# Cross attention of a two-layer decoder: the value products in two blocks a row, with eight exponential tiles, another order of the small products between the score rounds, and a last row on two score banks

## Chip, cores and metric

One core of one Trainium2 chip runs the whole program. The metric is device time in microseconds (us) of one execution. The kernel before took 1463.95 us (median of 3 runs, 1462.85 to 1476.16).

## What is computed

Two decoder layers over 16 batch rows of 112 tokens with 256 features. Each layer has a self attention (a different kind in each), a cross attention to a context of 375 x 128 a batch row, and a mixture of 8 experts. The change touches the cross attention alone, which runs once in each layer. Cut to what matters:

```python
qh = (layernorm(x) @ Wq + bq).reshape(B, 112, 16, 16)     # 16 heads of 16
kh = (ctx @ Wk + bk).reshape(B, 375, 16, 16)
vh = (ctx @ Wv + bv).reshape(B, 375, 16, 16)
attn = softmax(einsum('bqhd,bkhd->bhqk', qh, kh) / sqrt(16), axis=-1)
x = x + einsum('bhqk,bkhd->bqhd', attn, vh).reshape(B, 112, 256) @ Wo + bo
logits = layernorm(x) @ Wr + br                            # for the experts that follow
```

All of it is in float32.

## The kernel before

`cross_attention` (line 577) handles one batch row after another, t = 0 to 15, as a hand-written pipeline. Every engine has its own loop over t from -3 to 17 or so, and semaphores tie them together; what an engine does in a row stands in a fixed order, so an instruction that waits holds back all that is behind it on that engine.

The 16 heads of a row are taken in 8 slots of 2 heads. In each slot TensorE (PE) runs one *round* (`round_of`, L713): the two score products of a row ahead (`score`, L704, 112 x 375 into the bank pair `bsc`), from which VectorE (DVE) takes the maximum (`maximum`, L975); and the six products of the present row that compute the scores again, transposed and already shifted by that maximum (`shifted_score`, L710, into the bank pair `bp`), from which ScalarE (ACT) takes the exponential (`exps`, L892) into a tile `p`. Scores run 3 slots beyond a row ahead (`ahead`): slot 5 of row t has the first scores of row t + 2. There is one `bsc` and one `bp`, so a round waits until the maximum and the exponential of the round before have read them:

```python
reused(pe, exped, PAIRS * t + slot)      # L718
...
reused(pe, maxed, r - 1 if r < FILL else r)   # L725
```

Between two rounds stands a *gap* of other PE work, gap 0 behind round 0 and so on (L841 to L885). The value products of a row (`values`, L753: 12 small products for 4 heads, into `bo`) come in four blocks of one quad each; in gaps 2, 4 and 6 of their row and in gap 0 of the next, because there are only four `p` tiles. The other gap work is: the key projections `keys` (L785, two a row, bank `bk`), `queries` (L792, bank `bx`), the three `context_values` (L804), transposes of the normed row (`x_turn`, L761), of the negated maxima (`shift_turn`, L810), of the value sums (`u_turn`, L816), of the divided output (`out_turn`, L822) and of the new row (`row_turn`, L769), the output projection (`out_product`, L828) and the router's `logits` (L775). In gap 0 `keys` waits for `lg_set` (L781), which DVE raises in `row_logits` (L1038) when it has read the logits out of `bk`; in DVE's order that comes behind the first maximum of the row.

Three DMA transfers from SyncE (SP) join the engines: the keys of two rows ahead (`spread_k`, L653), the queries of two rows ahead (`spread_q`, L662 and L664, behind `q_copy`, L989, on DVE), whose end the round of slot 5 waits for (L721), and the negated maxima of the next row (`spread_nm`, L671), whose end round 0 of the next row waits for (L717).

In row 15 no scores are left, so a round has the six shifted products alone. Behind it, in t = 16 and 17, follow the last value block, the division, the output projection, the new row and its logits, and then the next phase.

Of the kernel before, what the change touches and what calls it, by code (L numbers as in the profile page):

```python
# [84 lines left out]
def reused(eng, sem, n):  # L85

    if not isinstance(n, int) or n > 0:
        eng.wait_ge(sem, n)
# [488 lines left out]
def cross_attention(nc, g, layer, xn_dram):  # L577
# [10 lines left out]
    qT = ph.sb("qT", [P, RB, QUADS, S])  # L588
    zeros = ph.sb("zeros", [4, QUADS, S])
    vb = ph.sb("v", [CT, VB, NC3, H, HD + 1])  # L590
    p = [ph.sb(f"p{u}", [CT, 2, NC3 * S]) for u in range(4)]
    mx = ph.sb("mx", [S, 2, 4, QUADS])
    nm = ph.sb("nm", [S, H])
    nmT = ph.sb("nmT", [H, 2, S])
# [33 lines left out]
    def on(b):  # L628
        return 0 <= b < NB
# [4 lines left out]
    def score_banks(b, pair):  # L634

        r = PAIRS * b + pair
        return bp if r < FILL and r % 2 else bsc

    def ahead(t, slot):
        return (t + 1, slot + 3) if slot < 5 else (t + 2, slot - 5)  # L640

    with nc.Block() as block:
# [53 lines left out]
        def _(pe):  # L696
# [10 lines left out]
            def shifted_score(b, pair, i, c):  # L707
                j, n = head(pair, i)
                r = 32 * j
                return pe.matmul(bp[0:CT, i, c * S:(c + 1) * S], kT[r:r + 32, b % RB, n, c * CT:(c + 1) * CT],  # L710
                                 qT[r:r + 32, b % RB, n, :], start=True, stop=True)

            def round_of(t, slot):  # L713
                sb, sp = ahead(t, slot)
                if on(t):
                    if slot == 0:
                        pe.wait_ge(nm_spread[t % RB], 16 * NM_DMAS * (t // RB + 1))  # L717
                    reused(pe, exped, PAIRS * t + slot)  # L718
                if on(sb):
                    if sp == 0:  # L720
                        pe.wait_ge(q_spread[sb % RB], 16 * Q_DMAS * (sb // RB + 1))  # L721
                    if sp % 4 == 0:
                        pe.wait_ge(k_spread[RB * (sp // 4) + sb % RB], 16 * K_DMAS * (sb // RB + 1))
                    r = PAIRS * sb + sp
                    reused(pe, maxed, r - 1 if r < FILL else r)  # L725
                if on(t):
                    for i in range(2):
                        shifted_score(t, slot, i, 0)
                if on(sb):
                    score(sb, sp, 0)  # L730
                    score(sb, sp, 1).then_inc(scored, 1)
                if on(t):
                    for c in range(1, NC3):
                        for i in range(2):
                            last = shifted_score(t, slot, i, c)
                    last.then_inc(shifted, 1)
                elif on(sb):
                    if sb == 0 and sp == 0:
                        pe.wait_ge(br_set, 1)
                    idle_products(bm[:, 0:P], 1)  # L740

            def values(b, n):
                pe.wait_ge(exped, PAIRS * b + 2 * n + 2)
                if n == 0:
                    reused(pe, u_copied, b)
                    pe.wait_ge(v_copied, NC3 * (b + 1))
                    if b == 0:
                        pe.wait_ge(set_v, 2 - layer)
                        pe.wait_ge(v_set, 1)
                for c in range(NC3):  # L750
                    for j in range(4):
                        slot = 2 * n + j // 2
                        last = pe.matmul(bo[32 * j:32 * j + HD + 1, n * S:(n + 1) * S], vb[:, b % VB, c, 4 * n + j, :],  # L753
                                         p[slot % 4][:, j % 2, c * S:(c + 1) * S], start=(c == 0), stop=(c == NC3 - 1))
                last.then_inc(valued, 1)

            def x_turn(b):
# [54 lines left out]
            def u_turn(b):  # L812
                pe.wait_ge(u_copied, b + 1)
                reused(pe, x_summed, b)
                for n in range(QUADS):
                    last = pe.transpose(bm[0:S, n * P:(n + 1) * P], uT[:, n * S:(n + 1) * S], g.ident[:, :])  # L816
                last.then_inc(u_turned, 1)
# [19 lines left out]

            if layer == 0:
                pe.wait_ge(g.cross_in, 16 * CROSS_DMAS)
            keys(0, 0)  # L840
            for t in range(-3, NB + 2):  # L841
                round_of(t, 0)
                if on(t - 1):
                    values(t - 1, 3)
                if on(t + 2) and t > -2:
                    keys(t + 2, 0)
                round_of(t, 1)
                if on(t + 2):
                    queries(t + 2)
                    if t == -2:  # L850
                        bias_rows()
                        idle_products(bp[:, 0, 0:P], 5 + 4 * layer)
                round_of(t, 2)
                if on(t):
                    values(t, 0)
                if on(t - 1):
                    u_turn(t - 1)
                round_of(t, 3)
                if on(t + 1):
                    context_values(t + 1, 0)  # L860
                    context_values(t + 1, 1)
                round_of(t, 4)
                if on(t):
                    values(t, 1)
                if on(t + 1):
                    context_values(t + 1, 2)
                round_of(t, 5)
                if on(t + 2):
                    keys(t + 2, 1)
                if on(t + 1):  # L870
                    shift_turn(t + 1)
                round_of(t, 6)
                if on(t):
                    values(t, 2)
                if on(t - 1):
                    out_turn(t - 1)
                if on(t - 2):
                    row_turn(t - 2)
                round_of(t, 7)
                if on(t + 3):  # L880
                    x_turn(t + 3)
                if on(t - 1):
                    out_product(t - 1)
                if on(t - 2):
                    logits(t - 2)  # L885

        @block.scalar
        def _(act):
            def exps(t, slot):
                act.wait_ge(shifted, PAIRS * t + slot + 1)  # L890
                reused(act, valued, 4 * t + slot // 2 - 1)
                act.activation(p[slot % 4][:, :, :], bp[0:CT, :, 0:NC3 * S], ACT.Exp).then_inc(exped, 1)  # L892

            def x_copy(b):
                act.wait_ge(x_turned, b + 1)
# [40 lines left out]
            for t in range(-3, NB + 2):  # L936
                if on(t):
                    exps(t, 0)
                if on(t - 1):
                    u_copy(t - 1)  # L940
                if on(t + 2):
                    k_copy(t + 2, 0)
                for slot in (1, 2, 3):
                    if on(t):
                        exps(t, slot)
                if on(t + 1):
                    v_copy(t + 1, 0)
                    v_copy(t + 1, 1)
                if on(t):
                    exps(t, 4)  # L950
                if on(t + 1):
                    v_copy(t + 1, 2)
                if on(t):
                    exps(t, 5)
                if on(t + 2):
                    k_copy(t + 2, 1)
                if on(t + 1):
                    shift_copy(t + 1)
                if on(t):
                    exps(t, 6)  # L960
                if on(t - 1):
                    out_copy(t - 1)
                if on(t - 2):
                    row_copy(t - 2)
                if on(t):
                    exps(t, 7)
                if on(t + 3):
                    x_copy(t + 3)

        @block.vector  # L970
        def _(dve):
# [73 lines left out]
            for t in range(-3, NB + 3):  # L1045
                for slot in range(8):
                    sb, sp = ahead(t, slot)
                    if on(sb):
                        maximum(sb, sp)
                    if slot == 0 and on(t - 3):  # L1050
                        row_logits(t - 3)
                    if slot == 0 and on(t - 2):
                        finish(t - 2)
                    if slot == 1 and on(t + 2):
                        q_copy(t + 2)
                        if t == -2:
                            bias_copies()
                    if slot == 2 and on(t - 1):
                        normalise(t - 1)
                    if slot == 3 and on(t - 2):  # L1060
                        second_norm(t - 2)
                    if slot == 4 and on(t + 1):
                        shift_rows(t + 1)
                    if slot == 6 and on(t + 3):
                        normed_row(t + 3)
                        if t == -3:
                            first_tiles()
# [900 lines left out]
```

## Time and profile before

| what | value |
|---|---|
| median of 3 runs | 1463.95 us (1462.85, 1463.95, 1476.16) |
| span of the profiled execution | 1473.2 us, TensorE clock 0.911 in the mean |
| its own time | 1476.16 us, the only one of the three above its span |
| cross attention of layer 0 | first round of row 0 at 197.2 us, last logits read at 491.9 us |
| cross attention of layer 1 | first round of row 0 at 972.1 us, last logits read at 1277.2 us |
| busy over the whole span | PE 89%, DVE 48%, ACT 38%, POOL 30% |

The span is the time from the first to the last instruction. A timeline row gives start, duration, engine, line, operation, tiles and count; what stands in brackets is how long the engine had stood idle and what ended that. One float32 product is two MATMUL records. PE records overlap, so a group's own duration says less than the distance from its start to the start of what follows.

### The profile page before, as it was taken

The page shows a single profiled execution, that of the slowest core. Times are in us where ns is not written, and L with a number is a line of the kernel's source. Part 1 is how long each engine was busy: PE and PEld are TensorE (multiplying, and loading weights), DVE is VectorE, ACT ScalarE, POOL GpSimd, SP SyncE. Part 2 cuts the span into 40 slices and gives each one's busy share as a digit, 9 for nine tenths or more (in the row PEclk, how much of TensorE's full clock was granted, in tenths as well). Part 3 has the DMA queues.
Part 4 walks back from the last instruction along what each step waited for, and adds up shares of the span by engine and source line. Part 5 has one row for each costly group of instructions (what it writes and reads, how often), then busy time and mean ns, then how long its engine had stood idle before and what let it go on. Part 6 is the DMA issues. An engine that isn't in the chain of part 4 may idle for free. (4 is left out here: it accounts for less than half of the span.)

```text
span 1473.2 us, 34595 instructions
## 1 busy us (share of the span) xinstructions
PE 1305.0 (89%) x13568; PEld 1036.2 (70%) x13568; DVE 701.9 (48%) x1744; ACT 558.2 (38%) x1246; POOL 444.8 (30%) x654
## 2 busy tenths in 40 slices
PE   5998899999998389999994999799999998559996
PEld 2665457777776279999993777557777776459996
DVE  4885345555552612222222999545565552323322
ACT  2776035555554012222221555135555553112221
POOL 5994300000000155556552221200000000135662
PEclk8999579999998589999997999799999997569999
DMA  7000111111110369999984000011111110279994
GB/s 241 2 2 2 23 26 36 36 36 37 36 36 17 128 225 340 346 347 337 329 320 107 1 1 1 15 29 42 44 44 43 42 43 25 80 192 347 356 368 147
DMA packets 61355, 177.89 MB, mean 121 GB/s; under 512 B 20608, under 2 KB 41953, under 8 KB 46756
## 3 DMA queue, kind: packets, MB, share of 16 engines
q0 software_dynamic: 22176, 141.55, 27.0%
q1 hardware_dynamic: 39044, 34.46, 9.2%
q8 instruction: 95, 1.56, 0.4%
q14 instruction: 40, 0.33, 0.1%
HBM read 147.62 MB, written 12.85 MB: 109 GB/s over the span
## 5 line engine op out<-in xcount | busy, mean ns | idle before, releaser
L975 DVE TENSOR_REDUCE xa_mx<-xa_ps_s 112x2 f32<-112x750 f32 x246 | 231.5, 941 | 219.4 <-PE xa_ps_s L704 215.9
L892 ACT ACTIVATE xa_p<-xa_ps_p 125x672 f32<-125x672 f32 x256 | 187.2, 731 | 236.2 <-PE xa_ps_p L710 236.2
L710 PEld LDWEIGHTS xa_ps_p<-xa_qT,xa_kT 32*125 32x125 f32 x3072 | 199.4, 191 | 95.3 <-ACT xa_p L892 66.8
L710 PE MATMUL xa_ps_p<-xa_qT,xa_kT 32*125 32x112 f32 x3072 | 243.4, 291 | 24.4 <-DVE xa_mx L975 10.4
L704 PE MATMUL xa_ps_s<-xa_kT,xa_qT 32*112 32x375 f32 x984 | 224.8, 534 | 1.0 <-DMA xa_qT<-xa_qU 1.0
L1803 PEld LDWEIGHTS ex_ps_h<-ex_xT,ew_w 128*128 128x128 f32 x1792 | 213.7, 196 | 4.8 <-issue 2.0
L1803 PE MATMUL ex_ps_h<-ex_xT,ew_w 128*128 128x128 f32 x1792 | 214.3, 279 | 1.3 <-ACT ex_xT L1833 1.3
L1814 PE MATMUL ex_ps_y<-ew_w,ex_hT 128*128 128x256 f32 x896 | 202.7, 379 | 0.0
L1814 PEld LDWEIGHTS ex_ps_y<-ew_w,ex_hT 128*128 128x128 f32 x896 | 165.9, 190 | 20.2
L1837 ACT ACTIVATE ex_hT<-ex_ps_h,ew_w 128x128 f32<-128x128 f32 x224 | 70.1, 364 | 282.5 <-PE ex_ps_h L1803 282.5
L1849 DVE TENSOR_SCALAR ex_hT<-ex_ps_h,ew_w 128x128 f32<-128x128 f32 x224 | 68.2, 346 | 163.7 <-PE ex_ps_h L1803 163.7
L1090 POOL TENSOR_SCALAR rstd<-mv 112x1 f32<-112x1 f32 x32 | 7.1, 221 | 418.5 <-DVE mv L1015 418.5
L753 PE MATMUL xa_ps_o<-xa_p,xa_v 125*17 125x112 f32 x3072 | 103.5, 270 | 0.0
L571 POOL TENSOR_TENSOR line_inv<-line_ss,nhalf 112x32 f32<-112x32 f32 x16 | 87.7, 5478 | 9.5 <-DVE line_ss L476 9.3
L753 PEld LDWEIGHTS xa_ps_o<-xa_p,xa_v 125*17 125x17 f32 x3072 | 68.9, 100 | 14.7 <-issue 1.2
L785 PE MATMUL xa_ps_k<-cT,wk_x 128*128 128x375 f32 x128 | 60.7, 558 | 15.3 <-DVE lg L1038 11.0
L704 PEld LDWEIGHTS xa_ps_s<-xa_kT,xa_qT 32*112 32x112 f32 x984 | 68.7, 174 | 5.0 <-issue 3.5
L1095 POOL TENSOR_TENSOR x<-x,crow 112x256 f32<-112x256 f32 x16 | 11.6, 726 | 191.2 <-DVE xa_xn L178 191.2
L1868 DVE TENSOR_TENSOR ex_y<-ex_ps_y,ew_w 128x256 f32<-128x256 f32 x35 | 14.8, 424 | 109.0 <-PE ex_ps_y L1814 89.5
L1740 POOL DMA_INDIRECT ex_xg<-xn,ex_now x56 | 55.7, 994 | 23.1 <-issue 21.4
L903 ACT ACTIVATE xa_kU<-xa_ps_k,bk_x 128x375 f32<-128x375 f32 x64 | 36.7, 574 | 48.4 <-PE xa_ps_k L785 48.3
L1833 ACT ACTIVATE ex_xT<-ex_ps_t 128x256 f32<-128x256 f32 x56 | 21.5, 384 | 79.9 <-PE ex_ps_t L1791 79.9
(304 smaller groups left out, 2000.0 us busy)
## 6 DMA issues: line engine op xcount, KB each, us to landing
xa_kT<-xa_kU SPq DMA_DIRECT2D x128, 93.8 KB, 2.2
xa_qT<-xa_qU SPq DMA_DIRECT2D x64, 56.0 KB
xn<-xa_x SPq DMA_DIRECT2D x32, 112.0 KB, 2.2
lin_yg<-ys SPq DMA_DIRECT2D x16, 224.0 KB, 5.2
cT<-in_ctxT SPq DMA_DIRECT2D x4, 750.0 KB, 8.3
xa_qT<-xa_nmT SPq DMA_DIRECT2D x128, 1.8 KB
x<-in_x SPq DMA_DIRECT2D x4, 448.0 KB, 6.2
xn<-x SPq DMA_DIRECT2D x16, 112.0 KB, 2.1
```

Source lines behind the costliest of these rows:

```text
L571: pool.tensor_tensor(inv[:, b % 2], ss[:, b % 2], g.nhalf[:, :], ALU.pow).then_inc(inv_done, 1)
L704: return pe.matmul(score_banks(b, pair)[0:S, i, 0:CL], qT[r:r + 32, b % RB, n, :], kT[r:r + 32, b % RB, n, :], start=True, stop=True)
L710: return pe.matmul(bp[0:CT, i, c * S:(c + 1) * S], kT[r:r + 32, b % RB, n, c * CT:(c + 1) * CT], qT[r:r + 32, b % RB, n, :], start=True, s ...
L753: last = pe.matmul(bo[32 * j:32 * j + HD + 1, n * S:(n + 1) * S], vb[:, b % VB, c, 4 * n + j, :], p[slot % 4][:, j % 2, c * S:(c + 1) * S] ...
L785: pe.matmul(bk[:, 0:CL], g.wk_x[:, layer, m * P:(m + 1) * P], g.cT[:, b, :], start=True, stop=True).then_inc(k_made, 1)
L892: act.activation(p[slot % 4][:, :, :], bp[0:CT, :, 0:NC3 * S], ACT.Exp).then_inc(exped, 1)
L975: dve.tensor_reduce(mx[:, b % 2, j:j + 2, n], score_banks(b, pair)[0:S, :, 0:CL], AX, ALU.max).then_inc(maxed, 1)
L1740: pool.indirect_dma_start(xg[:, slot, :], None, xn_dram, bass.IndirectOffsetOnAxis(ap=now[:, slot, 0:1], axis=0)) \
L1803: last = pe.matmul(bh[k][:, (j % 2) * SLOTS:(j % 2 + 1) * SLOTS], w[:, u, (1 - c) * FF + j * P:(1 - c) * FF + (j + 1) * P], xT[:, 1 - c, : ...
L1814: last = pe.matmul(by[u % 2][:, 0:D], hT[:, u % 2, j, :], w[:, u, 2 * FF + FJ + j * D:2 * FF + FJ + (j + 1) * D], start=(j == 0), stop=(j ...
L1837: last = act.activation(hT[:, u % 2, 2 * k + i, :], bh[k][:, i * SLOTS:(i + 1) * SLOTS], ACT.Relu, bias=bias(u, 2 * k + i))
L1849: last = dve.tensor_scalar(hT[:, u % 2, 2 * k + i, :], bh[k][:, i * SLOTS:(i + 1) * SLOTS], bias(u, 2 * k + i), 0.0, ALU.add, ALU.max)
```

## The change

- There are eight `p` tiles, one for each slot, so `values` and `exps` use `p[slot]`, and an exponential waits for the value products of the row before in its slot.
- The four value blocks of a row come in two pairs: quads 0 and 1 in gap 6 of the row, quads 2 and 3 in gap 1 of the next.
- The rest is spread over the other six gaps: `keys(t+2, 0)` and `x_turn(t+2)` in gap 0 (the transpose was in gap 7 for row t + 3), `queries` in gap 2 (was 1), `u_turn` in gap 4 (was 2), `shift_turn`, `keys(t+2, 1)` and `out_turn` in gap 5 (`out_turn` was in 6), `row_turn` in gap 6, `out_product` and `logits` in gap 7. ACT's copies follow in that order.
- DVE does `row_logits` ahead of the first maximum of a row, `q_copy` in slot 2 (was 1), `normalise` in slot 4 (was 2).
- Row 15 has an order of its own (`last_row`): its rounds use `bp` and `bsc` in turn, and come in pairs.

```diff
-    p = [ph.sb(f"p{u}", [CT, 2, NC3 * S]) for u in range(4)]
+    p = [ph.sb(f"p{u}", [CT, 2, NC3 * S]) for u in range(PAIRS)]
...
+    def shift_banks(b, pair):
+
+        return bsc if b == NB - 1 and pair % 2 else bp
...
-                    reused(pe, exped, PAIRS * t + slot)
+                    if t < NB - 1 or slot == 0:
+                        reused(pe, exped, PAIRS * t + slot)
+                    elif slot == 1:
+                        pe.wait_ge(maxed, PAIRS * NB)
+                    else:
+                        pe.wait_ge(exped, PAIRS * t + slot - 1)
...
+            def last_row(t):
+                round_of(t, 0)
+                round_of(t, 1)
+                values(t - 1, 2)
+                values(t - 1, 3)
+                round_of(t, 2)
+                round_of(t, 3)
+                values(t, 0)
+                u_turn(t - 1)
...
                 round_of(t, 0)
-                if on(t - 1):
-                    values(t - 1, 3)
                 if on(t + 2) and t > -2:
                     keys(t + 2, 0)
+                if on(t + 2):
+                    x_turn(t + 2)
                 round_of(t, 1)
+                if on(t - 1):
+                    values(t - 1, 2)
+                    values(t - 1, 3)
+                round_of(t, 2)
                 if on(t + 2):
                     queries(t + 2)
...
                 round_of(t, 6)
                 if on(t):
-                    values(t, 2)
-                if on(t - 1):
-                    out_turn(t - 1)
+                    values(t, 0)
+                    values(t, 1)
...
-                reused(act, valued, 4 * t + slot // 2 - 1)
-                act.activation(p[slot % 4][:, :, :], bp[0:CT, :, 0:NC3 * S], ACT.Exp).then_inc(exped, 1)
+                reused(act, valued, 4 * (t - 1) + slot // 2 + 1)
+                act.activation(p[slot][:, :, :], shift_banks(t, slot)[0:CT, :, 0:NC3 * S], ACT.Exp).then_inc(exped, 1)
...
+                    if slot == 0 and on(t - 3):
+                        row_logits(t - 3)
                     if on(sb):
                         maximum(sb, sp)
-                    if slot == 0 and on(t - 3):
-                        row_logits(t - 3)
```

On PE, from gap 7 of a row in the middle of layer 0 to gap 1 of the next, before (the three rows `xa_ps_p`, `xa_ps_s`, `xa_ps_p` are a round; a group's name says what it writes and from what):

```order
L761 MATMUL xa_ps_x<-ident,xa_xn 128x112 x2
L828 MATMUL xa_ps_m<-wo_x,xa_aoT 112x256 x2
L775 MATMUL xa_ps_k<-wr,xa_x2T 112x8 x2
L710 MATMUL xa_ps_p<-xa_qT,xa_kT 125x112 x2
L704 MATMUL xa_ps_s<-xa_kT,xa_qT 112x375 x2
L710 MATMUL xa_ps_p<-xa_qT,xa_kT 125x112 x4
L753 MATMUL xa_ps_o<-xa_p,xa_v 17x112 x12
L785 MATMUL xa_ps_k<-cT,wk_x 128x375
L710 MATMUL xa_ps_p<-xa_qT,xa_kT 125x112 x2
L704 MATMUL xa_ps_s<-xa_kT,xa_qT 112x375 x2
L710 MATMUL xa_ps_p<-xa_qT,xa_kT 125x112 x4
L792 MATMUL xa_ps_x<-xa_xT,wq_x 128x112 x4
```

and the same stretch of the changed kernel:

```order
L837 MATMUL xa_ps_m<-wo_x,xa_aoT 112x256 x2
L784 MATMUL xa_ps_k<-wr,xa_x2T 112x8 x2
L714 MATMUL xa_ps_p<-xa_qT,xa_kT 125x112 x2
L708 MATMUL xa_ps_s<-xa_kT,xa_qT 112x375 x2
L714 MATMUL xa_ps_p<-xa_qT,xa_kT 125x112 x4
L794 MATMUL xa_ps_k<-cT,wk_x 128x375
L770 MATMUL xa_ps_x<-ident,xa_xn 128x112 x2
L714 MATMUL xa_ps_p<-xa_qT,xa_kT 125x112 x2
L708 MATMUL xa_ps_s<-xa_kT,xa_qT 112x375 x2
L714 MATMUL xa_ps_p<-xa_qT,xa_kT 125x112 x4
L762 MATMUL xa_ps_o<-xa_p,xa_v 17x112 x24
```

The transpose into `xa_ps_x` moved from gap 7 into gap 0, the value block left gap 0, a double one stands in gap 1, and the queries left gap 1.

On DVE, from the last slot of such a row to slot 3 of the next, before (`xa_mx` is the maximum, `lg` the logits, `xa_qU` the queries, `xa_rs` and `xa_ao` the division):

```order
L975 TENSOR_REDUCE xa_mx<-xa_ps_s 112x2 x2
L1038 TENSOR_TENSOR lg<-xa_ps_k,xa_brb 112x8
L1011 TENSOR_TENSOR x<-x,xa_ps_m 112x256
L1013 BN_STATS xa_stats<-x 112x6
L1015 BN_AGGR mv<-xa_stats 112x2
L975 TENSOR_REDUCE xa_mx<-xa_ps_s 112x2
L989 SCALAR_TENSOR_TENSOR xa_qU<-xa_ps_x,xa_bqs 128x224
L975 TENSOR_REDUCE xa_mx<-xa_ps_s 112x2
L1002 RECIPROCAL xa_rs<-xa_ps_m 112x16
L1004 TENSOR_TENSOR xa_ao<-xa_ps_m,xa_rs 112x256
```

and now:

```order
L1005 TENSOR_REDUCE xa_mx<-xa_ps_s 112x2
L1068 TENSOR_TENSOR lg<-xa_ps_k,xa_brb 112x8
L1005 TENSOR_REDUCE xa_mx<-xa_ps_s 112x2
L1041 TENSOR_TENSOR x<-x,xa_ps_m 112x256
L1043 BN_STATS xa_stats<-x 112x6
L1045 BN_AGGR mv<-xa_stats 112x2
L1005 TENSOR_REDUCE xa_mx<-xa_ps_s 112x2 x2
L1019 SCALAR_TENSOR_TENSOR xa_qU<-xa_ps_x,xa_bqs 128x224
```

The logits are read one maximum earlier, and the queries are copied one maximum later.

On PE, row 15 of layer 0, from its first round on, before (x6 is a round without scores):

```order
L710 MATMUL xa_ps_p<-xa_qT,xa_kT 125x112 x6
L753 MATMUL xa_ps_o<-xa_p,xa_v 17x112 x12
L710 MATMUL xa_ps_p<-xa_qT,xa_kT 125x112 x12
L753 MATMUL xa_ps_o<-xa_p,xa_v 17x112 x12
L816 MATMUL xa_ps_m<-ident,xa_uT 112x128 x4
```

and now:

```order
L714 MATMUL xa_ps_p<-xa_qT,xa_kT 125x112 x6
L714 MATMUL xa_ps_s<-xa_qT,xa_kT 125x112 x6
L762 MATMUL xa_ps_o<-xa_p,xa_v 17x112 x24
L714 MATMUL xa_ps_p<-xa_qT,xa_kT 125x112 x6
L714 MATMUL xa_ps_s<-xa_qT,xa_kT 125x112 x6
L762 MATMUL xa_ps_o<-xa_p,xa_v 17x112 x12
L825 MATMUL xa_ps_m<-ident,xa_uT 112x128 x4
```

Two rounds go to two banks back to back, where each waited for the exponential of the one before.

## Rows read from the trace of the kernel before

**Rows 1.** The page: busy time of each engine, and the group of the value products.

```profile
PE 1305.0 (89%) x13568; PEld 1036.2 (70%) x13568; DVE 701.9 (48%) x1744; ACT 558.2 (38%) x1246; POOL 444.8 (30%) x654
...
L753 PE MATMUL xa_ps_o<-xa_p,xa_v 125*17 125x112 f32 x3072 | 103.5, 270 | 0.0
```

**Rows 2.** Timeline of row 7 of layer 0: PE and DVE.

```profile
319.99 0.36 PE L710 MATMUL xa_ps_p<-xa_qT,xa_kT 32*125 32x112 f32 x2
...
322.09 0.87 PE L785 MATMUL xa_ps_k<-cT,wk_x 128*128 128x375 f32 x2 [0.50 <-DVE lg L1038]
...
322.89 0.36 PE L710 MATMUL xa_ps_p<-xa_qT,xa_kT 32*125 32x112 f32 x2
...
323.73 1.15 PE L792 MATMUL xa_ps_x<-xa_xT,wq_x 128*128 128x112 f32 x8
323.84 0.94 DVE L975 TENSOR_REDUCE xa_mx<-xa_ps_s 112x2 f32<-112x750 f32 x1 [0.89 <-PE xa_ps_s L704]
...
324.91 0.39 DVE L989 SCALAR_TENSOR_TENSOR xa_qU<-xa_ps_x,xa_bqs 128x224 f32<-128x224 f32 x1
324.93 0.36 PE L710 MATMUL xa_ps_p<-xa_qT,xa_kT 32*125 32x112 f32 x2
...
325.76 0.77 PE L753 MATMUL xa_ps_o<-xa_p,xa_v 125*17 125x112 f32 x24
...
326.46 0.65 PE L816 MATMUL xa_ps_m<-ident,xa_uT 128*112 128x128 f32 x4
327.04 0.36 PE L710 MATMUL xa_ps_p<-xa_qT,xa_kT 32*125 32x112 f32 x2
...
330.62 0.70 PE L804 MATMUL xa_ps_x<-wv_x,cT 128*125 128x256 f32 x2
...
331.24 0.36 PE L710 MATMUL xa_ps_p<-xa_qT,xa_kT 32*125 32x112 f32 x2
...
332.08 0.90 PE L785 MATMUL xa_ps_k<-cT,wk_x 128*128 128x375 f32 x2
...
332.82 0.26 PE L810 MATMUL xa_ps_x<-ident,xa_nm 112*16 112x112 f32 x1
...
333.28 0.36 PE L710 MATMUL xa_ps_p<-xa_qT,xa_kT 32*125 32x112 f32 x2 [0.20 <-DVE xa_mx L975]
...
334.82 0.41 PE L822 MATMUL xa_ps_m<-ident,xa_ao 112*128 112x112 f32 x2
...
335.35 0.36 PE L710 MATMUL xa_ps_p<-xa_qT,xa_kT 32*125 32x112 f32 x2
...
336.44 1.03 PE L828 MATMUL xa_ps_m<-wo_x,xa_aoT 128*112 128x256 f32 x4
...
337.70 0.36 PE L710 MATMUL xa_ps_p<-xa_qT,xa_kT 32*125 32x112 f32 x2
```

**Rows 3.** Timeline of SP: issues of the query transfers in rows 6 and 7.

```profile
308.23 2.01 SPq L664 DMA_DIRECT2D xa_qT<-xa_qU  x2
...
325.94 1.29 SPq L664 DMA_DIRECT2D xa_qT<-xa_qU  x2
```

**Rows 4.** The tile of the keys: its transfers, from issue to landing.

```profile
DMA to landing us min/median/max: 2.0/2.2/3.3
```

**Rows 5.** Timeline of row 15 in both layers: first round, last value block.

```profile
460.19 0.91 PE L710 MATMUL xa_ps_p<-xa_qT,xa_kT 32*125 32x112 f32 x12
...
479.43 1.32 PE L753 MATMUL xa_ps_o<-xa_p,xa_v 125*17 125x112 f32 x24
...
1240.24 1.60 PE L710 MATMUL xa_ps_p<-xa_qT,xa_kT 32*125 32x112 f32 x12
...
1264.73 1.32 PE L753 MATMUL xa_ps_o<-xa_p,xa_v 125*17 125x112 f32 x24
```

**Rows 6.** Stretches: busy time of PE, PEld, DVE, ACT, POOL; granted clock; DMA.

```profile
462.00:485.00 23.00, 18.84 (x206) 14.43 (x207) 3.12 (x10) 7.50 (x13) 1.23 (x3) 0.66 0.04 11
...
1245.00:1275.00 30.00, 23.68 (x201) 18.17 (x201) 4.62 (x15) 6.76 (x12) 1.56 (x4) 0.50 0.06 16
```

More of the change, by code:

```diff
@@ L709, in shifted_score @@
                 r = 32 * j
-                return pe.matmul(bp[0:CT, i, c * S:(c + 1) * S], kT[r:r + 32, b % RB, n, c * CT:(c + 1) * CT],
+                return pe.matmul(shift_banks(b, pair)[0:CT, i, c * S:(c + 1) * S], kT[r:r + 32, b % RB, n, c * CT:(c + 1) * CT],
                                  qT[r:r + 32, b % RB, n, :], start=True, stop=True)
@@ L753, in values @@
                         last = pe.matmul(bo[32 * j:32 * j + HD + 1, n * S:(n + 1) * S], vb[:, b % VB, c, 4 * n + j, :],
-                                         p[slot % 4][:, j % 2, c * S:(c + 1) * S], start=(c == 0), stop=(c == NC3 - 1))
+                                         p[slot][:, j % 2, c * S:(c + 1) * S], start=(c == 0), stop=(c == NC3 - 1))
                 last.then_inc(valued, 1)
@@ L839, in _ @@
                 pe.wait_ge(g.cross_in, 16 * CROSS_DMAS)
+            def last_row(t):
[7 more added lines that the diff above has]
+                u_turn(t - 1)
+                round_of(t, 4)
+                round_of(t, 5)
+                values(t, 1)
+                out_turn(t - 1)
+                row_turn(t - 2)
+                round_of(t, 6)
+                round_of(t, 7)
+                out_product(t - 1)
+                logits(t - 2)
             keys(0, 0)
             for t in range(-3, NB + 2):
+                if t == NB - 1:
+                    last_row(t)
+                    continue
                 round_of(t, 0)
-                if on(t - 1):
-                    values(t - 1, 3)
                 if on(t + 2) and t > -2:
                     keys(t + 2, 0)
+                if on(t + 2):
+                    x_turn(t + 2)
                 round_of(t, 1)
+                if on(t - 1):
+                    values(t - 1, 2)
+                    values(t - 1, 3)
+                round_of(t, 2)
                 if on(t + 2):
@@ L852, in _ @@
                         idle_products(bp[:, 0, 0:P], 5 + 4 * layer)
-                round_of(t, 2)
-                if on(t):
-                    values(t, 0)
-                if on(t - 1):
-                    u_turn(t - 1)
                 round_of(t, 3)
@@ L862, in _ @@
                 round_of(t, 4)
-                if on(t):
-                    values(t, 1)
+                if on(t - 1):
+                    u_turn(t - 1)
                 if on(t + 1):
@@ L867, in _ @@
                 round_of(t, 5)
+                if on(t + 1):
+                    shift_turn(t + 1)
                 if on(t + 2):
                     keys(t + 2, 1)
-                if on(t + 1):
-                    shift_turn(t + 1)
+                if on(t - 1):
+                    out_turn(t - 1)
                 round_of(t, 6)
                 if on(t):
-                    values(t, 2)
-                if on(t - 1):
-                    out_turn(t - 1)
+                    values(t, 0)
+                    values(t, 1)
                 if on(t - 2):
@@ L879, in _ @@
                 round_of(t, 7)
-                if on(t + 3):
-                    x_turn(t + 3)
                 if on(t - 1):
@@ L938, in _ @@
                     exps(t, 0)
+                if on(t + 2):
+                    k_copy(t + 2, 0)
+                    x_copy(t + 2)
+                if on(t):
+                    exps(t, 1)
                 if on(t - 1):
                     u_copy(t - 1)
-                if on(t + 2):
-                    k_copy(t + 2, 0)
-                for slot in (1, 2, 3):
+                for slot in (2, 3):
                     if on(t):
@@ L954, in _ @@
                     exps(t, 5)
+                if on(t + 1):
+                    shift_copy(t + 1)
                 if on(t + 2):
                     k_copy(t + 2, 1)
-                if on(t + 1):
-                    shift_copy(t + 1)
                 if on(t):
@@ L966, in _ @@
                     exps(t, 7)
-                if on(t + 3):
-                    x_copy(t + 3)
         @block.vector
@@ L1047, in _ @@
                     sb, sp = ahead(t, slot)
+                    if slot == 0 and on(t - 3):
+                        row_logits(t - 3)
                     if on(sb):
                         maximum(sb, sp)
-                    if slot == 0 and on(t - 3):
-                        row_logits(t - 3)
                     if slot == 0 and on(t - 2):
                         finish(t - 2)
-                    if slot == 1 and on(t + 2):
+                    if slot == 2 and on(t + 2):
                         q_copy(t + 2)
@@ L1057, in _ @@
                             bias_copies()
-                    if slot == 2 and on(t - 1):
-                        normalise(t - 1)
                     if slot == 3 and on(t - 2):
@@ L1063, in _ @@
                         shift_rows(t + 1)
+                    if slot == 4 and on(t - 1):
+                        normalise(t - 1)
                     if slot == 6 and on(t + 3):
```

## Prediction

> **What bounds the kernel now.** I read the page first, then the stretches, then the timeline of one row, then the tails of the phase and the transfers. The page has PE busy in 89% of the span and the next engine, DVE, in 48% [rows 1]; PE records overlap, so that is no proof that PE sets the pace of the cross attention. The timeline of row 7 does that. The row lasts 337.70 - 319.99 = 17.71 us [rows 2]. In two slots the next round comes 2.04 us after the one before (322.89 to 324.93, 331.24 to 333.28), and the second of these says what PE waited for: the maximum on DVE, 0.20. The loop is: round start, 0.95 until the maximum starts (322.89 to 323.84), 0.94 of maximum, 0.15 until PE goes on. With one bank pair for scores no slot can be shorter, so the floor of a row is 8 x 2.04 = 16.32 us. The row is 17.71 - 16.32 = 1.39 above it. Where: a gap begins 0.84 after its round (322.89 to 323.73), so gap work up to 1.20 is free and what is over it is paid. Gap 0 pays 2.90 - 2.04 = 0.86 (a value block, then `keys`, which stood idle 0.50 for the logits to be read on DVE). Gap 2 pays 0.07 (324.93 to 327.04), gaps 3 and 4 together 0.12 (327.04 to 331.24), gap 6 0.03, gap 7 0.31 (335.35 to 337.70).
>
> **The row, gap by gap.** The pieces, start to start [rows 2]: a value block 0.70 (325.76 to 326.46), `u_turn` 0.58, the third context product 0.62, a key projection 0.74 (332.08 to 332.82), `shift_turn` 0.26 (0.46 to the round less 0.20 of waiting), `out_turn` and `row_turn` together 0.53 (334.82 to 335.35), `out_product` with `logits` 1.26 (336.44 to 337.70). A transpose pair, `x_turn` too, I put at half of 0.53, 0.27.
>
> A pair of value blocks is not in the trace. The block's group lasts 0.77 and one of its products 0.27 [rows 1, 2], so the last of 24 records starts 0.50 after the first, and the 0.20 from there to the next instruction is what a change of form costs. A second block of the same form could then start after 0.52, and the pair takes 0.52 + 0.70 = 1.22; I take 1.24. The other end is two full blocks, 1.40.
>
> - Gap 0: 0.74 + 0.27 = 1.01, free: 2.04. The wait for the logits goes, because DVE reads them ahead of the maximum of slot 0, some 0.9 earlier, while PE is in round 0. `keys` is late next, behind its own round.
> - Gap 1: 0.84 + 1.24 = 2.08. DVE's sums of slot 0 follow the maximum as before and now end close to the next maximum; I add 0.01 for them: 2.09.
> - Gap 2, `queries`: 2.04, as it had in gap 1. Gap 3 unchanged: 2.04. Gap 4: 0.84 + 0.58 + 0.62 = 2.04.
> - Gap 5: 0.84 + 0.26 + 0.74 + 0.27 = 2.11. Gap 6: 0.84 + 1.24 + 0.27 = 2.35. Gap 7: 0.84 + 1.26 = 2.10.
>
> Sum: 2.04 x 4 + 2.09 + 2.11 + 2.35 + 2.10 = 16.81, against 17.71: 0.90 a row. Rows 3 to 12 of both layers have this pattern, 20 x 0.90 = 18.0. Rows 0 to 2 and 13 lack parts of the work that is moved; for these 8 I take half, 3.6. Together 21.6 us. With pairs of 1.40 it would be 0.32 x 28 = 9.0 less.
>
> The ACT and DVE orders I cost at nothing. ACT is busy in 38% of the span [rows 1], its copies stand between two exponentials as before, at most two in a slot, and where a round waited in row 7 it was for DVE, not for ACT [rows 2]; without that cover a late exponential would hold the next round by what it is late. `normalise` on DVE, now behind the maximum of slot 4, has 2.04 - 0.94 = 1.10 until the next maximum, and if it needed more, it is the maximum of slot 5 that would start late. The eight `p` tiles add a wait on value products that ended a slot or more before. The transfer of the negated maxima is issued earlier in the row, as `shift_turn` stands first in gap 5 and the key copy behind it.
>
> **The edit that adds a risk.** The queries move one slot later, but the round of slot 5 waits for their transfer as before; behind that wait stand all of PE's rounds. `q_copy` starts 1.18 after the queries (323.73 to 324.91) [rows 2], now 0.84 + 1.18 = 2.02 after round 2. Round 5 comes 3 x 2.04 = 6.12 after round 2, so 4.10 is left from `q_copy` to the landing; before it was 331.24 - 324.91 = 6.33. The first of the two query transfers is issued 1.03 after `q_copy` (325.94), the second half of 1.29 later, at 1.68 [rows 3]. The trace gives no landing for them; the keys' transfers take 2.0 to 3.3, 2.2 in the middle [rows 4]. So the landing is at 3.7 to 5.0, most likely 3.9: 0.2 to spare, or at the worst 0.9 late in each of 28 rows, 25 us. I take the middle, since most transfers lie near it, with 2 us for the late ones (row 6 issued its pair in 2.01 instead of 1.29, 0.7 later).
>
> **Row 15.** From its first round to its last value block layer 0 took 479.43 - 460.19 = 19.24 and layer 1 1264.73 - 1240.24 = 24.49 [rows 5]. A round of six products took 0.91 at first in layer 0 and 1.60 in layer 1, a value block 1.32 at both ends against 0.77 in row 7: the granted clock is 0.66 in the first tail and 0.50 in the second [rows 6], that is 1.2 GHz in part of the one and in all of the other. Now: four pairs of rounds, each 0.64 + 0.84 = 1.48, 5.9; three value stretches, 1.24 + 0.70 + 0.70, and 0.52 to the last block, 3.2; `u_turn` 0.58, the transposes 0.53, projection and logits 1.26. That is 11.4 of PE work at 2.4 GHz, and I add 1.5 for waits on exponentials and copies: 12.9. At 1.2 GHz PE work grows by 1.60 / 0.91 = 1.76, to 20, and hides the waits. So layer 0 gains between 6.3 and -0.8 (I take 4) and layer 1 in this execution between 11.6 and 4.5 (I take 7).
>
> **Sum.** Profiled execution: 21.6 - 2 + 4 + 7 = 30.6, from 1476.2 to 1445.6. The median lies 12.2 below it, and 5.2 of that may be the slow tail of layer 1 (24.49 - 19.24); for the median I take 4 for that tail as well: 21.6 - 2 + 4 + 4 = 27.6, 1463.95 - 27.6 = 1436. That is what I predict; its own range is 1428 to 1446.
>
> **The rivals.**
> 1. *The pair of blocks saves no change of form* (1.40): 9 us less, 1445. For it: no such pair stands in the trace. Against: inside a block the records start about 0.02 apart.
> 2. *The queries land late.* For it: only 0.2 to spare. Against: the middle landing fits. With 0.5 in every row 14 us instead of 2 go, 1448.
> 3. *The clock falls earlier in the tail.* Row 14 has no keys and no queries left, so its gaps 0 and 2 are now empty, where before gap 0 still had a value block; layer 1's tail stood at 1.2 GHz [rows 6]. Then row 15 gains nothing over layer 0's 19.24 (-0.8 each instead of 4), and row 14 takes up to 5 longer in each layer (as layer 1's row 15 did): 19.6 - 11.6 = 8, 1456. The Trainium skill ("TensorE: Matmul & The Clock Gate", section "Why this matters for your kernels") says that idle gaps between bursts of products send the clock to half. By that rule this rival would be the likely one, with its 1456. Against it stands row 7, where a value block takes 0.77, the speed of 2.4 GHz, with waits of 0.2 to 0.5 around it: short waits alone do not do it.
> 4. *Slower.* If the query pair is issued as in row 6 (0.7 later) and lands as the slowest of the key transfers (3.3), round 5 waits 5.7 - 4.1 = 1.6 in 28 rows, 45 us: 1463.95 - 29.6 + 45 = 1479. It decides from a wait of about 1.05 in every row, where all other gains are eaten. Against it: the slow issue is one row of many.
>
> That the change does not do what it says can be left out: the order of PE shows it.
>
> **Chances.** Forecast 0.61, rival 1 0.10, rival 2 0.12, rival 3 0.13, rival 4 0.04. About 1% (14.6 us) is what a measurement here can tell from no change, so faster means under 1449. The forecast and rival 1 count as faster, and about two thirds of rival 2: 0.79. Rival 3 and the rest of 2 are within 1%: 0.17. Rival 4 is slower: 0.04. The range, 1420 to 1457, reaches from a median run with both tails at full clock and no late landing (29.6 - 8 + 12.6 = 34 gained) and some 10 more for what I left out, to rival 3.
>
> **What would show it.** Row 7 of layer 0 lasts 16.8; no PE wait on the reading of the logits; slot 5 without an idle time ended by the query transfer; a group of 48 value records followed after 1.24; gap 6 the longest, 2.35; row 15 in about 13 where the clock is full. A row near 17.3 with waits on the transfer in slot 5 would be rival 2; rows of 16.8 with a total near 1455 would be rival 3.

## The result, and the profile after

The changed kernel took 1410.53 us (median of 5 runs, 1405.75 to 1427.47), the kernel before 1465.19 (median of 5, 1462.85 to 1476.16). The ratio is 0.963, 95% interval 0.960 to 0.967, a gain of some 54 us. Ratios compare, here and below, those runs of each kernel that lie within 1.5% of its fastest. The forecast was 1436.0 with a range from 1420 to 1457: the direction was right, and the gain about twice the 28 forecast. The time lies below the range.

The profiled execution of the changed kernel took 1427.47 us, with a span of 1425.8. It is the longest of its five, as the profiled execution before (1476.16) is the longest of its own, and both have their filling ahead of row 0 of layer 0 at 1.2 GHz (the last part below), so the two profiles are like with like: 1473.2 - 1425.8 = 47.4 us of span. The page, busy time of each engine and the group of the value products, answers to [rows 1]:

```profile
PE 1264.5 (89%) x13568; PEld 1023.8 (72%) x13568; DVE 701.8 (49%) x1744; ACT 555.1 (39%) x1246; POOL 445.6 (31%) x654
...
L762 PE MATMUL xa_ps_o<-xa_p,xa_v 125*17 125x112 f32 x3072 | 86.4, 260 | 0.0
```

As many instructions are run (x13568, x1744, x1246), PE is busy 40 us less, and its share of the span is 89% in both. The page alone says nothing of where the time went. The timeline of PE, DVE and SP in row 7 of layer 0, beside [rows 2, 3], says it for a row:

```profile
318.34 0.36 PE L714 MATMUL xa_ps_p<-xa_qT,xa_kT 32*125 32x112 f32 x2
...
318.44 0.17 DVE L1068 TENSOR_TENSOR lg<-xa_ps_k,xa_brb 112x8 f32<-112x8 f32 x1 [0.41 <-PE xa_ps_k L784]
...
319.17 0.90 PE L794 MATMUL xa_ps_k<-cT,wk_x 128*128 128x375 f32 x2
...
320.37 0.36 PE L714 MATMUL xa_ps_p<-xa_qT,xa_kT 32*125 32x112 f32 x2
...
321.21 1.34 PE L762 MATMUL xa_ps_o<-xa_p,xa_v 125*17 125x112 f32 x48
...
322.48 0.36 PE L714 MATMUL xa_ps_p<-xa_qT,xa_kT 32*125 32x112 f32 x2
...
324.50 0.39 DVE L1019 SCALAR_TENSOR_TENSOR xa_qU<-xa_ps_x,xa_bqs 128x224 f32<-128x224 f32 x1
324.52 0.36 PE L714 MATMUL xa_ps_p<-xa_qT,xa_kT 32*125 32x112 f32 x2
...
325.53 1.28 SPq L668 DMA_DIRECT2D xa_qT<-xa_qU  x2
...
328.58 0.36 PE L714 MATMUL xa_ps_p<-xa_qT,xa_kT 32*125 32x112 f32 x2
...
330.62 0.36 PE L714 MATMUL xa_ps_p<-xa_qT,xa_kT 32*125 32x112 f32 x2
...
331.45 1.34 PE L762 MATMUL xa_ps_o<-xa_p,xa_v 125*17 125x112 f32 x48
...
333.07 0.36 PE L714 MATMUL xa_ps_p<-xa_qT,xa_kT 32*125 32x112 f32 x2
...
335.26 0.36 PE L714 MATMUL xa_ps_p<-xa_qT,xa_kT 32*125 32x112 f32 x2
```

The row lasts 335.26 - 318.34 = 16.92. The logits are read at 318.44, ahead of the maximum, and the keys at 319.17 start without an idle time. The pair of value blocks is followed by the next round 1.27 after its start. Round 5 at 328.58 stands without an idle time too, 4.08 after the copy of the queries: no wait on their transfer in this row. Over the rows of both layers PE does wait for it three times, 2.2 us in all and 1.4 at the longest; before, no round of a row did:

```profile
PE xa_ps_p L714 <- DMA xa_qT<-xa_qU: 2.2, 3, 1.4
```

Gap 6 (2.45) and gap 7 (2.19) are the two long ones.

The stretches of the two tails say where the larger part went. Columns: busy time of PE, PEld, DVE, ACT, POOL, granted clock (1.00 is 2.4 GHz, 0.50 is 1.2 GHz), DMA share, GB/s. Before, row 14 and row 15 of layer 0, then of layer 1 (row 15 here to the end of its last value block):

```profile
443.80:460.19 16.39, 14.14 (x236) 11.02 (x235) 6.89 (x13) 8.04 (x15) 0.79 (x2) 1.00 0.11 28
460.19:480.75 20.56, 17.82 (x233) 13.96 (x232) 3.22 (x11) 7.10 (x11) 0.79 (x2) 0.72 0.02 6
1219.44:1240.24 20.80, 18.55 (x237) 14.15 (x236) 6.89 (x13) 8.15 (x15) 0.78 (x2) 0.77 0.13 33
1240.24:1266.06 25.82, 23.32 (x233) 18.28 (x232) 3.20 (x11) 7.11 (x11) 0.77 (x2) 0.50 0.04 10
```

After, row 14 of layer 0, then row 15 and what follows it up to the last logits, layer 0 and layer 1:

```profile
436.82:453.27 16.45, 13.73 (x236) 11.13 (x236) 6.89 (x13) 8.14 (x15) 0.79 (x2) 1.00 0.07 18
453.27:465.21 11.94, 11.18 (x257) 9.39 (x256) 3.31 (x11) 6.45 (x11) 0.79 (x2) 1.00 0.05 12
465.21:474.28 9.07, 4.00 (x23) 2.99 (x22) 2.78 (x9) 1.51 (x4) 1.58 (x4) 0.91 0.09 25
...
1208.44:1220.38 11.94, 11.18 (x257) 9.38 (x256) 3.30 (x11) 6.45 (x11) 0.77 (x2) 1.00 0.09 24
1220.38:1230.70 10.32, 5.27 (x22) 3.80 (x22) 2.77 (x9) 1.51 (x4) 1.57 (x4) 0.65 0.15 44
```

Row 15 took 20.56 and 25.82 at a clock of 0.72 and 0.50, and takes 11.94 at 1.00 in both layers: it never leaves 2.4 GHz now. A pair of its rounds, from the first round to the value products behind the second, takes 454.43 - 453.27 = 1.16:

```profile
453.27 0.58 PE L714 MATMUL xa_ps_p<-xa_qT,xa_kT 32*125 32x112 f32 x6
...
454.43 1.34 PE L762 MATMUL xa_ps_o<-xa_p,xa_v 125*17 125x112 f32 x48
```

Summed over the two profiles, both layers:

| stretch | before | after | gain |
|---|---|---|---|
| rows 3 to 12 | 177.10, 177.10 | 169.35, 169.47 | 15.4 |
| rows 0 to 2 and 13 | 69.48, 70.28 | 68.94, 68.96 | 1.9 |
| row 14 | 16.39, 20.80 | 16.45, 16.44 | 4.3 |
| row 15 | 20.56, 25.82 | 11.94, 11.94 | 22.5 |
| from there to the last logits | 11.16, 11.14 | 9.06, 10.32 | 2.9 |
| filling ahead of row 0 | 44.15, 30.08 | 44.18, 28.82 | 1.2 |

That is 48 us, and outside the cross attention each stretch is within 1.3 us of before. Of it 17.3 come from the rows and 30 from the tail (rows 14, 15 and what follows).

### The profile page after: what moved, and what is told of

Its sections match the earlier page's. It is cut to its first block and busy times, and to the rows that moved or that the text cites. A ratio compares the mean times of both kernels' runs of the same rounds, so it can differ in the third digit from the quotient of the medians.

```text
span 1425.8 us, 34587 instructions
## 1 busy us (share of the span) xinstructions
PE 1264.5 (89%) x13568; PEld 1023.8 (72%) x13568; DVE 701.8 (49%) x1744; ACT 555.1 (39%) x1246; POOL 445.6 (31%) x654
## 5 line engine op out<-in xcount | busy, mean ns | idle before, releaser
L921 ACT ACTIVATE xa_p<-xa_ps_p 125x672 f32<-125x672 f32 x248 | 181.3, 731 | 212.2 <-PE xa_ps_p L714 212.2
L714 PE MATMUL xa_ps_p<-xa_qT,xa_kT 32*125 32x112 f32 x2976 | 227.1, 282 | 25.7 <-DVE xa_mx L1005 10.5
L714 PEld LDWEIGHTS xa_ps_p<-xa_qT,xa_kT 32*125 32x125 f32 x2976 | 187.4, 184 | 77.2 <-ACT xa_p L921 59.3
L762 PE MATMUL xa_ps_o<-xa_p,xa_v 125*17 125x112 f32 x3072 | 86.4, 260 | 0.0
L1125 POOL TENSOR_TENSOR x<-x,crow 112x256 f32<-112x256 f32 x16 | 11.6, 725 | 181.7 <-DVE xa_xn L178 181.7
```

The source lines that it names most:

```text
L714: return pe.matmul(shift_banks(b, pair)[0:CT, i, c * S:(c + 1) * S], kT[r:r + 32, b % RB, n, c * CT:(c + 1) * CT], qT[r:r + 32, b % RB, n, ...
L921: act.activation(p[slot][:, :, :], shift_banks(t, slot)[0:CT, :, 0:NC3 * S], ACT.Exp).then_inc(exped, 1)
```

## The experiments

**e1: the change without its last row.** Row 15 keeps the changed order of all other rows, on one bank.

```diff
-        return bsc if b == NB - 1 and pair % 2 else bp
+        return bp
...
-                if t == NB - 1:
-                    last_row(t)
-                    continue
```

> The changed kernel with row 15 in the general order and on one score bank, so the new order of rows 0 to 14 alone. Theory A (the tail gives the part that was not forecast, because row 15 on two banks is short and stays at 2.4 GHz): row 15 takes 16 to 20 instead of 11.9 from its first round to the end of its last value product, and the clock falls inside it or before; 1420 at the least, 1430 to 1436 if the clock falls as in the kernel before. Theory B (the extra gain lies in the rows or outside the cross attention): within 5 of the changed kernel's 1411.

Measured: 1446.08 (median of 4), ratio 0.983, 0.974 to 0.992. Rows 3 to 12 take 169.43 and 169.28, as in the changed kernel; row 15 takes 24.60 and 22.27:

```profile
437.21:461.81 24.60, 21.84 (x257) 17.29 (x256) 3.47 (x12) 7.00 (x11) 1.58 (x4) 0.62 0.02 6
1223.52:1245.79 22.27, 19.51 (x257) 15.59 (x256) 3.30 (x11) 7.00 (x11) 1.27 (x4) 0.69 0.05 13
```

The row gain stands by itself, and without the two banks row 15 falls to 1.2 GHz for part of its length; it first falls 2.4 us behind the first round in layer 0 and 8.0 us behind it in layer 1. So theory A holds, but both numbers were missed: row 15 is longer than the 16 to 20 expected, and the time is above 1430 to 1436. The timeline of its first rounds shows the wait that the two banks take away, an empty gap in which PE stands until the exponential has read the one bank:

```profile
437.21 0.91 PE L714 MATMUL xa_ps_p<-xa_qT,xa_kT 32*125 32x112 f32 x12
...
438.94 1.03 PE L714 MATMUL xa_ps_p<-xa_qT,xa_kT 32*125 32x112 f32 x12 [0.83 <-ACT xa_p L913]
```

PE stands idle for 24.60 - 21.84 = 2.76 there in all; in the changed kernel it is 11.94 - 11.18 = 0.76. Row 14 is the same in both, with an idle time of 16.45 - 13.73 = 2.72, and stays at 1.00 in both.

**e2: the last row alone.** The rows 0 to 14 in the order of before, with eight `p` tiles and row 15 on two banks in pairs (against the kernel before):

```diff
+            def last_row(t):
+                round_of(t, 0)
+                round_of(t, 1)
+                values(t - 1, 3)
+                round_of(t, 2)
+                round_of(t, 3)
+                values(t, 0)
+                u_turn(t - 1)
...
```

> The kernel before with eight exponential tiles and the new row 15 (two banks, rounds in pairs), its old order in rows 0 to 14. Theory A: rows 3 to 12 stay at 17.71, row 15 takes about 12 and the tail gains 18 to 26 of the 54 us: 1439 to 1447. Theory B: at most the 9 us that the two banks are worth at an equal clock: 1456 or more.

Measured: 1440.65 (median of 4), ratio 0.984, 0.974 to 0.993. Rows 3 to 12 take 177.12 and 177.11, as before. Row 15, in both layers:

```profile
445.75:458.16 12.41, 11.21 (x233) 9.23 (x232) 3.23 (x11) 6.46 (x11) 0.79 (x2) 1.00 0.04 11
1211.04:1223.44 12.40, 11.19 (x233) 9.22 (x232) 3.21 (x11) 6.45 (x11) 0.77 (x2) 1.00 0.10 30
```

So the two parts add up: by the ratios e1 gains 25 us and e2 24 on 1468.31, each give or take 13 or so, and the change 54. Within these intervals each part carries about half; the two profiles above give 17 us to the rows and 30 to the tail. The eight tiles cost nothing that shows in rows 3 to 12.

**e3: the logits behind the first maximum again**, all else as changed.

```diff
-                    if slot == 0 and on(t - 3):
-                        row_logits(t - 3)
                     if on(sb):
                         maximum(sb, sp)
+                    if slot == 0 and on(t - 3):
+                        row_logits(t - 3)
```

> The changed kernel with DVE reading the logits behind the first maximum of a row again, nothing else. If the wait on the logits in gap 0 was worth what the row's sum says, the keys start 0.5 to 1.3 later in gap 0 and rows 3 to 12 take 17.4 to 18.1 instead of 16.93: 15 to 30 us slower than the changed kernel. If the wait is hidden in the new order: 16.93 and no difference.

Measured: 1431.98 (one run). Rows 3 to 12 take 180.10 and 181.21, more than the 177.10 of before; row 15 stays at 11.94. The timeline of slot 0 of row 7, PE and DVE:

```profile
305.78 0.36 PE L714 MATMUL xa_ps_p<-xa_qT,xa_kT 32*125 32x112 f32 x2
...
306.73 0.94 DVE L1005 TENSOR_REDUCE xa_mx<-xa_ps_s 112x2 f32<-112x750 f32 x1 [1.25 <-PE xa_ps_s L708]
307.58 0.16 DVE L1068 TENSOR_TENSOR lg<-xa_ps_k,xa_brb 112x8 f32<-112x8 f32 x1
...
307.88 0.87 PE L794 MATMUL xa_ps_k<-cT,wk_x 128*128 128x375 f32 x2 [1.20 <-DVE lg L1068]
...
308.88 0.36 PE L714 MATMUL xa_ps_p<-xa_qT,xa_kT 32*125 32x112 f32 x2
```

Nothing stands ahead of the keys in gap 0 any more, so the whole wait shows: 1.20 idle, and the slot takes 3.10 instead of 2.03. In the new order one small instruction on DVE, moved past one maximum, is worth 18.07 - 16.94 = 1.1 us a row (the means over rows 3 to 12 of both layers), more than the whole row gain.

**e4: the kernel before, with the logits first.** The same two statements of before, exchanged.

```diff
-                    if on(sb):
-                        maximum(sb, sp)
                     if slot == 0 and on(t - 3):
                         row_logits(t - 3)
+                    if on(sb):
+                        maximum(sb, sp)
```

> The kernel before, with DVE reading the logits ahead of the first maximum of a row, nothing else. If that order is the main gain of a row: gap 0 falls from 2.90 to 2.3 to 2.4 and rows 3 to 12 take 17.1 to 17.2 instead of 17.71, 5 to 6 us a layer, 10 to 12 us in all (1452 to 1458 against 1465). If the placing of the value blocks is the gain of a row and the logits matter only in the new order: 17.5 to 17.7.

Measured: 1451.24 (median of 10, 1438.84 to 1473.50 and one of 2400.36 that nothing here explains), ratio 0.989, 0.984 to 0.994. Rows 3 to 12 take 172.55 and 172.90, 17.27 a row against 17.71, between the two expectations; slot 0 of row 7 is 2.37 instead of 2.90, and the keys follow the value block without an idle time:

```profile
304.71 0.36 PE L710 MATMUL xa_ps_p<-xa_qT,xa_kT 32*125 32x112 f32 x2
...
305.55 0.77 PE L753 MATMUL xa_ps_o<-xa_p,xa_v 125*17 125x112 f32 x24
...
306.25 0.90 PE L785 MATMUL xa_ps_k<-cT,wk_x 128*128 128x375 f32 x2
...
307.08 0.36 PE L710 MATMUL xa_ps_p<-xa_qT,xa_kT 32*125 32x112 f32 x2
```

So 4.4 of the 7.7 us that a layer's rows 3 to 12 gain come from these two lines in the old order already; the remaining 3.3, a third of a microsecond a row, are the pairs and the moved work. Row 15 (24.07 and 20.05, clock 0.56 and 0.74) gains nothing. The ratio stands for 9 to 23 us, and rows 3 to 12 of both layers make 8.8 of them.

**e5: one bank, with the empty gaps filled.** As e1, but in the empty gaps of rows 14 and 15 PE multiplies the identity into a bank that nobody reads at that point, so the result is untouched.

```diff
+            FILLS = {(NB - 2, 0): 4, (NB - 2, 2): 4, (NB - 1, 0): 3, (NB - 1, 2): 3, (NB - 1, 3): 3, (NB - 1, 4): 1, (NB - 1, 5): 2}
...
+                    idle_products(bsc[:, 0, 0:P], n)
...
```

> The row order of the changed kernel with the general order and one score bank in row 15 (as in the run of the general last row), and products of the identity whose results nobody reads in the empty gaps of rows 14 and 15; they leave the computation as it is. If PE's activity decides the clock there: 2.4 GHz until the end of row 15, which takes 16 to 17 instead of 22 to 25 with one bank, 12 to 16 us less than that run and still 8 to 10 more than the changed kernel. If the two banks themselves were the gain and the clock falls anyway: 22 to 25 and no gain.

Measured: 1419.41 (median of 4), ratio 0.972, 0.963 to 0.982. Row 15 in both layers:

```profile
434.76:451.55 16.79, 16.79 (x281) 14.10 (x280) 3.32 (x11) 6.99 (x11) 0.79 (x2) 1.00 0.04 10
1194.33:1211.12 16.79, 16.79 (x281) 14.11 (x280) 3.30 (x11) 6.99 (x11) 0.77 (x2) 1.00 0.06 17
```

PE has no idle time left and stays at 2.4 GHz, with the same bank, the same rounds and the same exponentials as e1. So PE's idle time is what let the clock fall. e5 fills gaps of row 14 too and does not part the two rows; but row 14 is unfilled in the changed kernel and in e1 alike, and only e1, with the waits of row 15 behind it, loses the clock. It also splits the gain of row 15: from e1's 24.60 and 22.27 to 16.79 is the clock, 7.8 and 5.5; from 16.79 to 11.94 is what the two banks and the pairs save at full clock, 4.85 (at most: the filling may overrun a gap; up to the fifth round it does not, as the rounds start 1.74, 3.85, 5.59 and 7.33 behind the first in e5 and in layer 1 of e1, which has 1.00 until then). Twice 4.85 is about the 9 us by which e5 is longer than the changed kernel. Against e1 it is 26.7 us shorter, more than the 12 to 16 expected: row 15 accounts for 13.3, the stretch behind it for 3.3, and the profiled execution of e1 has a long filling in layer 1 (last part), that of e5 has none.

**e6: two identity products in each filling round**, where the changed kernel has one, to hold the clock ahead of row 0.

```diff
-                    idle_products(bm[:, 0:P], 1)
+                    idle_products(bm[:, 0:P], 2)
```

> The changed kernel with two identity products instead of one behind each round of the fill ahead of row 0. If the spread of the runs is the clock in the two fills (28 to 30 us each at 2.4 GHz, 43 to 44 at 1.2): both fills at 28 to 31 in most runs, 1400 to 1408 and a smaller spread. If the clock there does not follow this work: the same spread and 1 to 4 us slower.

Measured: 1409.97 (median of 6, 1408.24 to 1416.02), ratio 0.965, 0.959 to 0.970; both fillings take 30 us (29.87 and 30.20). None of the six runs is near 1427, but four of the five runs of the changed kernel are as short, and the 1400 to 1408 expected were not reached. It is not shown to be faster than the changed kernel.

**e0 and e7: the two kernels once more.**

> The kernel before, once more with a profile. If its tail at 1.2 GHz is its rule and not a mishap of one execution, layer 1's row 15 again takes 24 to 26 from its first round to the end of its last value product, and layer 0's 19 to 26. If the first profile was an exception, 15 to 17 in both.

> The changed kernel once more with a profile. Row 15 at 11.9 in both layers and 2.4 GHz as before, rows 3 to 12 at 16.93; the fills at 28 to 44, apart from each other and from the first profile.

Measured: 1473.24 and 1412.78 (one run each). e0 has its long filling in layer 1 and not in layer 0:

```profile
155.18:185.99 30.81, 28.40 (x121) 16.06 (x121) 15.64 (x24) 4.73 (x12) 12.42 (x24) 0.81 0.12 28
933.79:977.35 43.56, 41.12 (x123) 21.77 (x124) 15.19 (x22) 4.38 (x11) 8.55 (x12) 0.54 0.10 22
```

Its row 15 takes 23.83 and 23.23, at a clock of 0.58 and 0.60: a little under the 24 to 26 expected of layer 1, and nowhere near 15 to 17, so the long tail is no exception. e7 has neither filling long (27.97 and 29.23), rows 3 to 12 at 169.39 and 169.44, and row 15 at 11.95 and 11.94. The tails of rows 14, 15 and what follows, both layers together, take 102.2 in e0 and 75.3 in e7: 27 us, where the two profiles gave 30.

## Why the prediction was right and wrong

- *The row.* Right in its working: 16.92 against 16.81 forecast, 0.77 gained a row against 0.90. The wait for the logits is gone, and e4 and e3 show that it was the largest single cause. The pair of value blocks takes 1.27 against 1.24, which refutes the first rival (1.40). The misses are gap 6, 2.45 against 2.35, gap 7, 2.19 against 2.10, and on the other side gap 5, 2.04 against 2.11. Rows 0 to 2 and 13 were taken at 3.6 and gave 1.9.
- *The queries.* The distance from the copy to round 5 was worked out as 4.10 and is 4.08, and in most rows nothing waits. A few transfers are late, as the prediction took it for 2 us: 2.2 us of waiting in the changed kernel, 0.4 to 2.3 in e1, e3, e5, e6 and e7. The longest waits, 1.4 in e3 and 1.65 in e6, are about the 1.6 of the fourth rival, but in one row of many and not in every one, so the second and the fourth rival do not happen.
- *The step that failed* is row 15: "layer 0 gains between 6.3 and -0.8 (I take 4) and layer 1 in this execution between 11.6 and 4.5 (I take 7)". The mechanism, pairs of rounds on two banks, was right. Wrong was the clock: I took a value between the two levels, as if the shorter row would run part of its length at 1.2 GHz as the longer one had. But the change takes away the idle time itself, 2.7 us of it down to 0.8, and e1 and e5 show that the clock hangs on it. All ten tails with the two-bank row (after, e2, e3, e6, e7) have row 15 at a clock of 1.00, in 11.94 to 12.41; all eight with one bank and empty gaps (before, e0, e1, e4) at 0.50 to 0.74, in 20 to 26. The end at 2.4 GHz was mis-sized as well: 12.9 to the start of the last value block, measured 11.2 (11.94 to the block's end). A pair of rounds was put at 1.48, with a 0.64 that no row shows, and takes 1.16; the waits, put at 1.5, are 0.76. In the two profiles the tail gave 30 us where 11 were taken: 7 more by the clock in row 15, 3.4 more by its work, and some 8 by what was put at nothing, row 14, the last value block and the stretch behind it. e0 and e7 give 27, where the forecast of the median took 8. With 27 in place of 8, and the rows at 17.3 for 19.6, the forecast would have been 1463.95 - 27.6 - 19 + 2.3 = 1420.
- *The third rival* had the same mechanism with the opposite sign. It feared the emptier gaps of row 14, and row 14 stays at 1.00 in both layers (16.45 and 16.44). The Trainium skill ("TensorE: Matmul & The Clock Gate", section "Why this matters for your kernels") warns of idle gaps between bursts of products, but of longer ones than the waits of these rows, 1.1 us at the most, so it did not make this rival the likely one. That several short waits can do it, other than I read from row 7, is what e1 and e5 show: 22.3 to 24.6 at 0.69 and 0.62 with the waits, 16.79 at 1.00 without. I looked for idle time only where the change adds it, and not where it takes it away.
- *The rest of the distance* is in the comparison of profile and median. I put part of the 12.2 us between them to the slow tail of layer 1, and took 3 less for the median's tail. The size was right, 105.9 for both tails in the first profile against 102.2 in e0, but it left the rest unexplained, and in e0 both layers have a long row 15 (23.83 and 23.23), so such a tail is nothing special to one execution. What differs more from one execution to the next, in both kernels, is the filling ahead of row 0 (last part). With a long one the profile of the changed kernel stands 16 us above the next longest of its runs.
- *The range* went down to "both tails at full clock", but priced that at 12.6 us, from layer 0's row 15 twice, and counted neither row 14 of layer 1 (4.4) nor the stretch behind row 15 (2.9).

What stays open: the last 9 us, from that 1420 to 1410.5 (the long filling may come more often before the change than after it; the profiles, with 2 long ones of 8 in the old order of the rows and 2 of 12 in the new, don't settle it); why row 14 falls to 0.77 in layer 1 of one execution of before and to 0.9 in both layers of e2 (18.08 and 17.94, with row 15 behind it at 1.00), and stays at 1.00 in e1, e7 and after; and which part of gaps 6 and 7 is the price of standing behind a pair.

## What to carry to other kernels

Where the granted clock falls in a stretch, ask first whether the change takes away the idle time of PE in that stretch. Here it did, and the end at full clock came, not a middle of the two levels. Idle time alone does not tell: row 14 of the changed kernel has as much of it as row 15 had, and keeps its clock. What an order that avoids a wait is worth depends on what else stands ahead of the waiting instruction: the same two lines were worth 0.4 to 0.5 us a row in the old order and about 1.1 in the new one. And before a profile is compared with a median, look which stretch of it is not the same in another execution.

## What was not expected of the hardware

The filling ahead of row 0 (the first keys, queries and scores, with PE busy for most of it) takes either 28 to 31 us or 43 to 44, with the same instructions: 44.15 and 30.08 in the two layers before, 44.18 and 28.82 after, 30.81 and 43.56 in e0, 27.94 and 43.15 in e1, 27.97 and 29.23 in e7, and 28 to 31 in both layers of e2 to e6. The stretches of after show that it is the clock, 0.50 against 0.85:

```profile
154.35:198.54 44.19, 43.03 (x120) 22.40 (x120) 15.68 (x24) 4.49 (x11) 12.43 (x24) 0.50 0.10 24
...
924.74:953.55 28.81, 26.59 (x121) 15.63 (x121) 15.13 (x22) 4.48 (x11) 8.56 (x12) 0.85 0.13 30
```

In this long one PE is busy for 43.03 of 44.19 us and is still left at 1.2 GHz throughout, so a busy engine alone does not raise the clock here; layer 0 of the first profile of the kernel before is the same (0.50). In e7, the same kernel as after, the clock is 0.50 in the first 7 us of layer 0's filling and 1.00 behind them. Why it comes back in the one and not in the other is open.

The long ones of layer 1 (e0 and e1, 0.54) are another case. In e0 the clock is 0.50 until 941.4, 1.00 from 941.6 to 944.8, and 0.50 again from 945.0 to the end of the filling. While it was up, PE waited for the first transfer of the queries, 1.68 us in e0 and 1.41 in e1; in the eight short ones of layer 1 this wait is 1.16 at the most. The lines of e0 and, short, of e3:

```profile
944.24 0.95 PE L704 MATMUL xa_ps_s<-xa_kT,xa_qT 32*112 32x375 f32 x4 [1.68 <-DMA xa_qT<-xa_qU]
...
929.58 0.89 PE L708 MATMUL xa_ps_s<-xa_kT,xa_qT 32*112 32x375 f32 x4 [1.16 <-DMA xa_qT<-xa_qU]
```

That the late transfer is the cause there is likely, but no run tests it. Long fillings come in either layer, in the old order of the rows and in the new, and one of them is about the 16 us by which the longest run of the changed kernel exceeds the next.
